# Fourth norm of rows 0 to 11 inside the last steps of the second attention, router logits of rows 8 to 15 by position, a new token-number product and a reordered down projection

## The reference

```python
x = x + L0_ffn(layernorm(x))         # quantised gate/up/down; the down product is its last step
x = x + L1_xattn(layernorm(x), ctx)  # 16 heads of 16; softmax(q k / 4) v, then out @ w_o.T + b_o
x = x + L1_ffn(layernorm(x))         # the mixture below

def L1_ffn(x):                                    # 2 groups of 1024 tokens, 8 experts, capacity 160
    probs = softmax(x @ w_router)                 # 256 -> 8
    gate, idx = top_k(probs, 2)
    pos = cumsum(one_hot(idx)) - 1                # place of a token in its expert's queue
    expert_in = gather(x, pos < 160)              # per expert 320 token rows
    h = relu(expert_in @ wi[e])                   # 256 -> 1024
    return scatter_add(gate * (h @ wo[e]))        # 1024 -> 256
```

## Time and profile before

| | |
|---|---|
| time before, median of 3 runs | 630.05 us (629.38 to 630.79) |
| the profiled execution, its own time | 631.85 us |
| its span, first to last instruction | 630.1 us |
| PE busy | 527.4 us, 84% |
| DVE busy | 390.2 us, 62% |
| ACT busy | 290.5 us, 46% |
| POOL busy | 153.7 us, 24% |
| mean granted TensorE clock | 0.937 |

### The profile page before, as it was taken

How to read it: one execution, slowest core, us unless ns; L and a number is a source line. 1 busy time by engine, 2 the same in 40 slices (tenths; PEclk the granted TensorE clock), 3 DMA queues, 4 the chain that set the end, 5 groups by cost and what they waited for, 6 DMA issues and landing times.

```text
span 630.1 us, 9662 instructions
## 1 busy us (share of the span) xinstructions
PE 527.4 (84%) x3406; PEld 374.7 (59%) x3406; DVE 390.2 (62%) x953; ACT 290.5 (46%) x556; POOL 153.7 (24%) x218
## 2 busy tenths in 40 slices
PE   1869999899899500798999999987499999999994
PEld 1548866644344200687757677765377777777773
DVE  5766789754389978778699799966623321333011
ACT  1526667633499868200268788864021122112220
POOL 2715533000000000002032232202024544354531
PEclk9969999999899855799999999999699999999998
DMA  8800000000000000430000011004015453544410
GB/s 236 275 1 2 2 1 1 2 0 1 0 0 0 1 1 0 143 124 1 1 1 2 1 36 35 2 34 167 5 32 175 128 192 114 173 142 164 127 47 21
DMA packets 30154, 37.59 MB, mean 60 GB/s; under 512 B 6560, under 2 KB 25888, under 8 KB 30112
## 3 DMA queue, kind: packets, MB, share of 16 engines
q1 hardware_dynamic: 27040, 29.07, 14.1%
q0 software_dynamic: 3072, 7.95, 4.4%
HBM read 30.14 MB, written 6.88 MB: 59 GB/s over the span
## 4 chain that ended last, share of the span: by engine, by line
PE 56%; DVE 25%; ACT 7%; issue 7%; SPq 1%; DMA 1%; DVEq 0%; POOL 0%; POOLq 0%; ACTq 0%
PE pA L1748 11%; PE pB L1766 9%; PE pC L1511 6%; DVE rm L1158 5%; PE pA L1473 3%; ACT arena L577 2%; PE pC L1759 2%; PE pC L1385 2%; PE pC L1473 2%; PE pB L1473 2%; DVE arena L1078 2%; DVE arena L1167 2%; PE pC L1723 1%; PE pA L1366 1%; DVE am L1011 1%
## 5 line engine op out<-in xcount | busy, mean ns | idle before, releaser
L457 POOL TENSOR_TENSOR arena<-KT,par 128x256 f32<-128x256 f32 x32 | 19.6, 634 | 256.6 <-DVE arena L1098 178.5
L1748 PE MATMUL pA<-arena 128*128 128x320 f32 x256 | 72.2, 436 | 0.9 <-ACT arena L765 0.9
L772 ACT ACTIVATE arena<-pA 128x320 f32<-128x320 f32 x64 | 28.0, 437 | 73.7 <-PE pA L1748 65.3
L1748 PEld LDWEIGHTS pA<-arena 128*128 128x128 f32 x256 | 48.0, 190 | 19.5 <-ACT arena L765 1.0
L1766 PE MATMUL pB<-arena 128*128 128x256 f32 x256 | 59.3, 385 | 0.0
L1766 PEld LDWEIGHTS pB<-arena 128*128 128x128 f32 x256 | 47.4, 190 | 9.4 <-issue 3.1
L1011 DVE TENSOR_REDUCE am<-arena 128x1 f32<-128x512 f32 (+1 forms) x48 | 32.0, 682 | 22.5 <-ACT arena L614 22.5
L1511 PE MATMUL pC<-wdnT,arena 128*128 128x256 f32 x192 | 42.9, 381 | 3.2 <-DVE arena L1098 3.2
L1511 PEld LDWEIGHTS pC<-wdnT,arena 128*128 128x128 f32 x192 | 36.0, 190 | 9.2 <-DVE arena L1098 4.2
L1296 PE MATMUL pB<-ident 128*128 128x128 f32 x80 | 14.3, 359 | 31.0 <-DVE arena L1078 31.0
L490 POOL DMA_INDIRECT arena<-token_rows,token x24 | 24.3, 1013 | 64.8 <-issue 33.7
(11 more groups left out here) (298 smaller groups left out, 1149.2 us busy)
## 6 DMA issues: line engine op xcount, KB each, us to landing
arena<-in_L_ffn_wi SPq DMA_DIRECT2D x8, 1024.0 KB
arena<-in_L_ffn_wo SPq DMA_DIRECT2D x8, 1024.0 KB, 5.8
X<-in_x SPq DMA_DIRECT2D x4, 512.0 KB, 5.8
arena<-in_ctx SPq DMA_DIRECT2D x4, 512.0 KB, 5.7
out<-X SPq DMA_DIRECT2D x4, 512.0 KB, 3.0
token_rows<-arena SPq DMA_DIRECT2D x4, 512.0 KB, 3.5
arena<-in_L_ffn_w_up SPq DMA_DIRECT2D x1, 768.0 KB, 8.9
arena<-in_L_ffn_w_gate SPq DMA_DIRECT2D x1, 768.0 KB, 10.3
```

Source lines behind the costliest of these rows:

```text
L772: nc.scalar.activation(HT[:, u, f, :], ps[2 + f % 2][:, 0:ROWS], ACT.Relu).then_inc(s["h_relu"], 1)
L1748: last = mm(ps[2 + f % 2][:, 0:ROWS], WI[:, u, k, f * P:(f + 1) * P], XET[:, u, k, :], start=(k == 0), stop=(k == KD - 1))
```

## The change

- The four loads of the attention's weights: `w_o` comes first, in four pieces, with its columns permuted in the transfer. The heads' output then needs no permutation, and `attn_out` is one instruction instead of two.
- In the down loop the wait for ACT inside `moments` goes: `variances` at t = 9 and 13, `inverse_roots` a step later. POOL's first `split_keys` waits for sixteen rounded rows instead of eight.
- The fourth norm of rows 0 to 11 moves into steps 16, 17 and 18 of the attention loop (DVE `norm4`, ACT `rsqrt(6, 12)`, `xt4(0)`, `xt4(1)`, PE `d_turn(0)`, `d_turn(1)`). The sixteen dummy matmuls ahead of `d_turn(0)` go. Only rows 12 to 15 are normed behind the loop.
- Logits of rows 0 to 7 are made as before. Those of rows 8 to 15 come straight in the layout that is wanted: `d_row`, per row two matmuls with 128 columns of X as stationary operand and eight columns of the router weight as moving one.
- POOL builds its tables without waiting for the attention's end, and clears its two buffers after the last `norm4`.
- `e_tokens` swaps its operands: the ids (32 columns) are stationary, the selection (192 columns) moves, in four column tiles. That is 16 matmuls. DVE copies the 128x384 result (`digits`), and `e_places`, four matmuls of one moving column, adds it up. `e_tokens(e + 1)` stands ahead of f = 1 and `e_places(e + 1)` ahead of f = 3 (for e = 0 ahead of f = 4 and f = 6).

```diff
+            for k in range(KD):
+                for e in range(2):
+                    sp.dma_start(LN[:, 3, k, :].rearrange("p (j e x) -> p j e x", j=4, e=2)[:, :, e],
+                                 A["L1_xattn_w_o"].rearrange("(k p) (e j x) -> k p e j x", p=P, e=2, j=4)[k, :, e]).then_inc(s["wo_in"], 16)
+            for n, nme in ((1, "k"), (2, "v"), (0, "q")):
...
-                    pool.wait_ge(s["oi_ready"], 8)
+                    pool.wait_ge(s["oi_ready"], NB)
...
-            pool.wait_ge(s["o_done"], NB)
-            nc.gpsimd.memset(XE[:, :, :, :], 0.0)
-            nc.gpsimd.memset(YG[:, :, :], 0.0)
...
+            pool.wait_ge(s["xr_ready"], NB // 2)
+            nc.gpsimd.memset(XE[:, :, :, :], 0.0)
+            link(nc.gpsimd.memset(YG[:, :, :], 0.0))
...
+                if t == NB + 2:
+                    xt4(1)
                 if 0 <= y < NB:
                     pt_copy(y, y % 2, 0)
+                if t == NB:
+                    rsqrt(6, 12)
...
                 if 0 <= o < NB:
                     os_copy(o, o % 2)
+                if t == NB + 1:
+                    xt4(0)
...
-            rsqrt(6, NB)
-            for p in range(6):
-                xt4(p)
-            lt_copy(0)
-            for p in range(6, 8):
-                xt4(p)
-            lt_copy(1)
+            xt4(2)
+            xt4(3)
+            rsqrt(7, 4, 12)
+            xt4(4)
+            xt4(5)
+            lt_copy()
+            xt4(6)
+            xt4(7)
...
                 if t == 9:
                     dve.wait_ge(s["row_stats"], NB + 8)
-                    moments(3, 8, D)
+                    variances(8, D)
+                if t == 10:
+                    inverse_roots(3, 8)
...
-                for e in range(2):
-                    last = V_.tensor_tensor(AO[:, u, :].rearrange("p (e j r d) -> p e j r d", e=2, j=4, r=2)[:, e], o.rearrange("p (j e r) d -> p e j r d", j=4, e=2)[:, e, :, :, 0:DH1],
-                                            rs[:, u, :].rearrange("p (j e r) -> p e j r", j=4, e=2)[:, e].unsqueeze(3).broadcast_to([P, 4, 2, DH1]), ALU.mult)
+                V_.tensor_tensor(AO[:, u, :].rearrange("p (h d) -> p h d", h=NH1), o[:, :, 0:DH1], rs[:, u, :].unsqueeze(2).broadcast_to([P, NH1, DH1]), ALU.mult).then_inc(s["ao_ready"], 1)
...
+            def norm4(p):
+                normed(XR[:, 2 * p, 0:D], 2 * p)
+                normed(XR[:, 2 * p + 1, 0:D], 2 * p + 1).then_inc(s["xr_ready"], 1)
             for t in range(NB + 4):
                 if 0 <= t - 4 < NB:
                     stats4(t - 4)
+                if t == NB:
+                    dve.wait_ge(s["row_stats"], 2 * NB + 12)
+                    variances(12, D)
+                    inverse_roots(6, 12)
+                    norm4(0)
+                if t == NB + 1:
+                    for p in (1, 2, 3):
+                        norm4(p)
+                if t == NB + 2:
+                    norm4(4)
+                    norm4(5)
...
             dve.wait_ge(s["row_stats"], 3 * NB)
-            moments(6, NB, D)
-            for p in range(NB // 2):
-                normed(XR[:, 2 * p, 0:D], 2 * p)
-                normed(XR[:, 2 * p + 1, 0:D], 2 * p + 1).then_inc(s["xr_ready"], 1)
+            variances(4, D, None, 12)
...
+            inverse_roots(7, 4, None, 12)
+            norm4(6)
+            norm4(7)
...
+            for q in range(2):
+                dve.wait_ge(s["d_row"], 4 * q + 4)
+                link(V_.tensor_copy(LW[:, 8 + 4 * q:12 + 4 * q, :], ps[5 + q][:, 0:4 * NE].rearrange("p (b e) -> p b e", b=4)))
...
+                V_.tensor_copy(digits[:, u, :], ps[7][:, 0:NG * SELW]).then_inc(s["id_kept"], 1)
+                dve.wait_ge(s["id_sum"], e + 1)
+                for n, c, c1 in ((P, 0, 2), (ROWS - 2 * P, 2, 3)):
+                    last = V_.tensor_scalar(token[0:n, cols(e, 1), c:c1].squeeze(1), ps[7][0:n, NG * SELW + c:NG * SELW + c1], float(NB * S), None, ALU.add)
...
-                if p == 0:
-                    keep_busy(ps[7], 16)
...
+            def d_row(b):
+                pe.wait_ge(s["d_xt"], b // 2 + 1)
...
+                for k in range(KD):
+                    last = mm(ps[5 + (b - 8) // 4][:, o:o + NE], KT[:, k, b * P:(b + 1) * P], wrt[:, k, :], start=(k == 0), stop=(k == KD - 1))
+                last.then_inc(s["d_row"], 1)
...
+            for p in range(2, 6):
                 d_turn(p)
+            d_logits()
+            for b in range(8, 12):
+                d_row(b)
             d_turn(6)
+            d_back()
             d_turn(7)
+            for b in range(12, NB):
+                d_row(b)
...
+                for b in range(NB):
+                    g, o = b // TG, 32 * (b % 4)
+                    if b % TG == 0:
+                        pe.wait_ge(s["sel_ready"], 2 * e + g + 1)
+                    last = mm(ps[7][o:o + 32, g * SELW:(g + 1) * SELW], ids[:, 2 * b:2 * b + 32], SEL[:, u, b, :],
+                              start=(b % TG < 4), stop=(b % TG >= 4))
...
+            def e_places(e):
+                u, o = e % 2, NG * SELW
+                pe.wait_ge(s["id_kept"], e + 1)
+                for c in range(2):
+                    mm(ps[7][:, o + c:o + c + 1], digits[:, u, c * SELW:c * SELW + P], pick[:, 0:1], start=True, stop=True)
+                mm(ps[7][0:SHORT, o + 2:o + 3], digits[:, u, P:SELW], pick[:, 0:1], start=True, stop=False)
+                mm(ps[7][0:SHORT, o + 2:o + 3], digits[:, u, SELW + P:2 * SELW], pick[:, 0:1], start=False, stop=True).then_inc(s["id_sum"], 1)
...
-                    if f == NFT // 2 and e + 1 < NE:
+                    early = 4 if e == 0 else 1
+                    if f == early and e + 1 < NE:
                         e_tokens(e + 1)
+                    if f == early + 2 and e + 1 < NE:
+                        e_places(e + 1)
```

110 lines of the change are left out of this document (53 added, 57 removed).

## The result

The changed kernel takes 620.34 us (median of 4 runs, 618.88 to 621.77) against 630.12 us (629.38 to 630.79) for the kernel before, run beside it: ratio 0.9837, 95% interval 0.9813 to 0.9861. It is 9.8 us faster, 0.8 us short of the forecast.

The account below looks back on a forecast made before the run. PE bounds the experts and mostly the down loop; attention, its end and the router are chains of waits. Terms -1.25 - 6.7 - 0.2 - 2.4 = -10.55 take the median 630.05 to 619.5 us; own range 616 to 624, 8 in 10: 615.8 to 625.0.

Parts of the forecast that it names:

- Down loop, -1.25: Down loop: row 10's rounding no longer waits for ACT and POOL's keys start later; saves 1.25 us, bounds 0.5 and 1.5.
- the 0.8: Down loop: PE's second wait, ahead of row 11, was to become about 0.8 us, as a sign of the forecast.
- Attention steps, 0: Attention loop: single attn_out leaves the 6.03 us period unchanged; its 0.25 us gain in the last steps is counted under router.
- Norm and router, -6.7: Attention's end to selection: norms moved into loop, d_row logits; selection at 435.8 against 442.49, saving 6.7 us, bounds 8.0 and 4.5.
- My split of the gain: Norm and router: of 6.7 us, about 4.1 from twelve norms leaving the path and 0.6 from POOL's clearing.
- DVE's idle at step 16: Attention step 16: DVE's 3.62 us wait, filled with moved norm work, was to shrink below 0.7 us.
- First expert's numbers, -0.2: Last selection to first expert's token number: 2.0 us against 2.2; saves 0.2, bounds +0.6 and -0.5.
- Experts, -2.4: Experts 0 to 6: new token product plus places 0.75 us against 1.09; 0.34 x 7 = 2.4 saved, bounds 3.4 and 0.6.
- The aside of 0.1: Experts: two more tile-shape changes per expert, estimated at 0.1 us each, would make the saving 1.4 us smaller.
- B: Router: without dummies the clock falls to 1.2 GHz, doubling PE's items; of 6.7 only 0.5 stays, 625.7 us; chance 0.08.
- C: Experts' token product: column tiles of bf16 do not overlap; 5.3 us lost instead of 2.4 won, 627.8 us; chance 0.06.
- D: Experts: late output-row gather delays DVE's copy, so PE waits at the places; 6 us late gives 645.7 us; chance 0.04.
- E: Whole kernel: in-loop norms delay add_attn by what they save and d_row costs its upper bound; about 630 us; chance 0.03.

Follow-up runs that it names:

- x4: Changed kernel with POOL's first masked keys after 8 rounded rows again; first down product to first row maxima 51.30 us, against 50.54.
- x5: Changed kernel with the third norm's factors in one piece again, DVE waiting for ACT; first down product to first row maxima 51.24 us, against 50.54.
- x6: Changed kernel with w_o loaded last and unpermuted, attn_out as two instructions again; sixteenth maxima to last addition 16.82 us, against 16.63.
- x8: Changed kernel with the whole fourth norm behind the attention loop, d_row kept, no dummies; 627.23 us, 0.9942 of the kernel before.
- x10: x8 with the sixteen dummy matmuls put back ahead of its turns; sixteenth maxima to selection 31.11 us, against 32.09 in x8.
- x3: Changed kernel with logits of rows 8 to 15 made by halves as before, no d_row; sixteenth maxima to selection 25.55 us, against 25.26.
- x9: Changed kernel with POOL's clearing started before the last norms, as before the change; sixteenth maxima to selection 25.25 us, against 25.26.
- x2: Changed kernel with the old token product, its place and DVE's reduction restored; first hidden to last output product 158.38 us (+0.76).
- x1: Changed kernel with expert 1's token product and places moved earlier, to f = 1 and 3; 618.98 us, 0.981 of the kernel before.
- x7: Kernel before the change without its sixteen dummy matmuls ahead of the turns; 634.56 us, ratio 1.0068.

## Why the prediction was right, point by point

- **Down loop, -1.25: right, -1.37.** Row 10's rounding starts 1.41 us earlier against the loop's start (1.3 forecast). From one rounding's start to the next went 3.29 us, where 2.49 + 0.81 = 3.30 was written, and to PE's start 1.26, where 1.27 was. PE's second wait is 0.43 and not 0.8; the 0.8 did not follow from the forecast's own starts, which leave 0.4, and the start of row 11 was right to 0.13. x4 and x5 show both halves.
- **Attention steps, 0: right** (-0.03; maxima 6.03 apart); x6 shows that `attn_out` is worth 0.19 in the tail.
- **Norm and router, -6.7: right in mechanism, 0.65 too much.** Counted from the sixteenth maxima, the four-row `variances` begin at 17.55 (forecast 17.5) and the last norms end at 21.07 (21.0). `d_logits` ends at 19.85, forecast 19.6 (ends by the start of the next instruction); rows 8 to 11 end 0.4 late and selection comes 0.64 late. The terms that were mis-sized are PE's and ACT's: a wait of 0.34 for ACT's copy ahead of turns 4 and 5, `d_row` at 0.45 to 0.49 us a row for 0.43, and copies and hops. My split of the gain, norms 4.1 of 6.7 and the clearing 0.6, does not hold: norms and turns in the loop carry 5.85 (x8, x10), `d_row` 0.29 (x3), and the clearing 0 (x9). They were sized one at a time as if each stood on the path. What an edit is worth hangs on the others: with the norms behind the loop the clearing is worth 0.5 and `d_row` costs 0.52.
- **DVE's idle at step 16, forecast below 0.7: missed.** It waits 1.12 for ACT, whose two small instructions stand behind copies. It had a wait of 3.62 to spend and the addition still came on time.
- **First expert's numbers, -0.2: -0.24, right as far as it can be told.** The dummies end when the rows are there, with no wait left, and x2 gives back 0.22. But kernels with the same code here lie at 20.27 to 20.47 us, and one at 20.80, against 20.55 to 20.59 with the old product, so the size is no surer than 0.1 or 0.2.
- **Experts, -2.4: the step that failed, -0.94.** Products at 0.45 + 0.28 = 0.73 instead of 0.75 are right. Two things weren't. Per expert the period went from 20.07 to 19.81, so 0.26 and not 0.34. The sum had two terms wrong that partly cancel: the old product is 1.19 from start to start and not 1.09, which would have made it 0.46, but the hidden products around the two new pieces take 0.19 longer than around the one old piece (9.00 for 8.81), for which the sum had no term. The aside of 0.1 for each of two further changes of tile shape has just this size; whether the changes or the interruptions as such cost it, no run shows. And for expert 0 I had taken the later place (f = 4 and 6) as harmless; it gives rows for expert 1 too late, 1.12 us of the 1.46 that were missing. x1 shows this: with the early place the stage gains 2.06.
- **Rivals.** B did not come: clock 1.00 up to 434. C did not: 16 instructions of 192 columns in 0.45 us. D did not: no wait before the places. E is excluded by the result. That x8 pays 0.98 us for a clock of 0.50, after 4.07 us without work on PE, shows that B's mechanism exists, and its doubling too: transposes of a turn start 0.21 us apart at 0.50 and 0.11 at 1.00. But B kept the clock low up to the selection, and in x8 it was back at 430.2 us, 3.4 us after the first turn began, so its price there was 0.98 us and not 6.2.
- **Side sums.** Two don't come out as written, and neither bears on the result. With `d_row` at 0.8 us a row the forecast's own chain ends at 438.8, so 3.7 would be saved and not 4.5, and at 0.2 it would be 8.3 and not 8.0. D decides at 4.1 us late with the experts' 2.4 still won, but prices 6 us late without them; with them it would be 643.3 and not 645.7.
- The medians differ by 9.8 us and the stages of the two profiles by 8.6. The rest would fit the spread before the down loop, but no run shows that it lies there. So the 0.8 us between forecast and median are partly luck: the stages alone fall 1.9 us short of the 10.55.

## What to carry to other kernels

Work that sits behind a loop is worth moving into the loop's last steps where the engine demonstrably waits: here twelve norms, with their factors, fitted into waits of 3.62, 2.27 and 1.80 us and brought nearly 6 us with the turns behind them, while the logits by position brought 0.3. Before dropping dummy matmuls, look whether other work fills the gap that they filled; the old kernel lost time without them, the new one did not. When a producer is moved, work out its deadline for the first iteration by itself, with the transfers that share the DMA engines at that time.

## What the hardware showed that was not expected

- The clock came back under transposes alone. In x8 the only PE instructions between 426.81 and 431.8 are transposes; the granted clock was 0.50 up to 430, 0.90 over 430 to 431 and 1.00 over 431 to 431.8. The Trainium skill (TensorE: Matmul & The Clock Gate, Part 4: PE-mode transpose) says that the full clock does not engage for PE's transposes, which don't count as busy in the same way as matmuls; here they sufficed to raise it, and the measurement decides.
- In x7 PE had waited 1.39 us ahead of the first turns and 0.85 us behind them, and the clock stood at 0.50 over 462 to 464; before, with 0.27 us and the same 0.85, it stood at 1.00 over 462 to 464.
- Two column tiles of 512 columns cost 1.05 us, four cost 1.06: fewer tiles saved nothing.
- An indirect gather's transfer took 5.10 us when a 1 MB load was issued 1.1 us ahead of it, and 2.55 us with no load beside it (expert 0 of the kernel before).
- 32 instructions of hidden products took 8.71 us in one stretch, 8.81 around one other product, and 9.00 around two.
- Small DVE instructions beside POOL's clearing of 128x768 were stretched from 0.17 to 0.81 us in the kernel before; in x9 it was one cast, from 0.35 to 0.71 us.
